# The first layer's image loop, with its barriers and semaphore clearing, written out as one block of straight code

## What is computed

```python
x_norm = _group_norm(x, gn_scale, gn_bias).reshape(b, seq, c)
qkv = x_norm @ w_qkv + b_qkv
q, k, v = jnp.split(qkv, 3, axis=-1)            # then to (b, 8, 1024, 64) each
weight = jax.nn.softmax(jnp.einsum('bhld,bhsd->bhls', q * scale, k * scale), axis=-1)
out = jnp.einsum('bhls,bhsd->bhld', weight, v)  # back to (b, 1024, 512)
out = out @ w_out + b_out
return (x_flat + out).reshape(b, h, w, c)
```

## Time and profile before

| | us |
|---|---|
| median of 3 runs | 4248.88 |
| the profiled execution | 4248.9 |
| its span (first to last instruction) | 4247.2 |
| VectorE busy | 2985.9 (70%) |
| ScalarE busy | 2580.8 (61%) |
| GpSimd busy | 1303.4 (31%) |

### The profile page before, as it was taken

The page is one execution under the profiler, slowest core; times in us unless marked ns, Lnnn a source line. Parts: engine busy times, 40 slices in busy tenths (PEclk is TensorE's granted clock), DMA queues, the critical chain, the costliest instruction groups (busy, mean ns, idle before and its releaser), DMA issues. The chain is left out here.

```text
span 4247.2 us, 65056 instructions
## 1 busy us (share of the span) xinstructions
PE 4062.9 (96%) x22762; PEld 3395.2 (80%) x22762; DVE 2985.9 (70%) x5141; ACT 2580.8 (61%) x5617; POOL 1303.4 (31%) x1423
## 2 busy tenths in 40 slices
PE   8999999999999999999999889999999999999999
PEld 6887878878878878788788577777777777777777
DVE  3983965956938839749569466859686868686866
ACT  3874855847828738558478136565656555555656
POOL 1431423432323324324323104132232314140504
PEclk9999999999999999999999989999999999999999
DMA  2221121221211211212211303031212121212212
GB/s 82 43 66 43 41 75 35 61 61 31 56 56 41 68 43 41 70 41 61 60 31 36 138 1 100 20 80 40 70 50 60 60 60 60 60 60 49 72 38 63
DMA packets 113159, 235.87 MB, mean 56 GB/s; under 512 B 17261, under 2 KB 33705, under 8 KB 112809
## 3 DMA queue, kind: packets, MB, share of 16 engines
q1 hardware_dynamic: 112808, 231.41, 20.4%
HBM read 80.35 MB, written 33.55 MB: 27 GB/s over the span
## 5 line engine op out<-in xcount | busy, mean ns | idle before, releaser
L599 DVE TENSOR_REDUCE a_neg_max<-a_ps 128x1 f32<-128x1024 f32 x512 | 624.7, 1221 | 337.1 <-PE a_ps L429 337.1
L558 ACT ACTIVATE a_ph<-a_ps 128x512 fp32r<-128x512 f32 x1024 | 556.9, 593 | 171.4 <-PE a_ps L443 168.5
L616 DVE TENSOR_TENSOR a_pl<-a_ps,a_ph 128x512 fp32r<-128x512 f32 x1024 | 654.2, 679 | 8.9 <-ACT a_ph L558 5.7
L565 ACT ACTIVATE a_prob<-a_ps,a_neg_max 128x1024 f32<-128x1024 f32 x512 | 572.3, 1118 | 17.5 <-DVE a_neg_max L599 11.8
L696 POOL TENSOR_TENSOR a_qk<-a_fold_s,a_fold_r 64x256 f32<-64x256 f32 x256 | 191.1, 747 | 1237.1 <-DVE a_fold_s L607 1237.1
L443 PEld LDWEIGHTS a_ps<-a_ident,a_prob 128*128 128x128 f32 x4096 | 469.8, 140 | 112.8 <-issue 47.0
L443 PE MATMUL a_ps<-a_ident,a_prob 128*128 128x128 f32 x4096 | 540.7, 274 | 17.3 <-DVE a_pl L616 16.2
L1697 POOL TENSOR_SCALAR b_prob<-b_prob,b_row_inv 128x256 f32<-128x256 f32 x512 | 246.7, 482 | 994.9 <-DVE b_row_inv L1606 959.0
L464 PE MATMUL a_ps<-a_ph,a_v 128*128 128x256 f32 x2048 | 550.7, 302 | 0.0
L464 PE MATMUL a_ps<-a_pl,a_v 128*128 128x256 f32 x2048 | 509.2, 282 | 0.0
L428 PE MATMUL a_ps<-a_kh,a_qs 128*128 128x512 f32 x1024 | 408.3, 399 | 11.9 <-POOL a_kl L687 11.9
(11 more groups left out here) (250 smaller groups left out, 9239.3 us busy)
## 6 DMA issues: line engine op xcount, KB each, us to landing
a_qs<-a_qk SPq DMA_DIRECT2D x128, 256.0 KB, 3.7
a_kl<-a_qk SPq DMA_DIRECT2D x128, 256.0 KB, 4.3
a_xtok<-in_x SPq DMA_DIRECT2D x64, 256.0 KB, 4.2
b_xs<-x SPq DMA_DIRECT2D x64, 256.0 KB, 4.6
b_qs<-b_qh SPq DMA_DIRECT2D x64, 256.0 KB, 3.0
b_qs<-b_ql SPq DMA_DIRECT2D x64, 256.0 KB, 3.8
b_z<-x SPq DMA_DIRECT2D x64, 256.0 KB, 3.2
out<-b_ot SPq DMA_DIRECT2D x64, 256.0 KB, 2.0
```

Of the source, the lines that this page charges most:

```text
L558: act.activation(ph[:, b % 2, 4 * g:4 * g + 4, (u % 2) * P:(u % 2 + 1) * P], ps[:, 4 + n % 2, :].rearrange("p (k q) -> p k q", k=4), ACT.C ...
L565: act.activation(prob[:, i_ % 2, :], ps[:, 2 * (i_ % 2):2 * (i_ % 2) + 2, :] .rearrange("p a b -> p (a b)"), ACT.Exp, bias=neg_max[:, i_:i ...
L599: dve.tensor_reduce(neg_max[:, i_:i_ + 1], ps[:, 2 * (i_ % 2):2 * (i_ % 2) + 2, :] .rearrange("p a b -> p (a b)"), AX, ALU.max, negate=Tru ...
L616: dve.tensor_tensor(pl[here], ps[:, 4 + n % 2, :].rearrange("p (k q) -> p k q", k=4), raw(ph[here]), ALU.subtract).then_inc(pl_ok, 1)
```

## The change

All eight images of the first layer stand in one block, each engine's list written out image by image. The functions of `image` become `sync_image(sp, r)`, `tensor_image(pe, r)` and so on, with a Python number `r` in place of the loop's register. The block's end per image (L364), the barrier with clearing per image (L716), the loop (L714) and the barrier behind the prologue (L360) are gone. The prologue's own block (and so its end, L262) stays, and so does the block's end and the clearing barrier behind the last image.

Semaphores are no longer cleared, so each wait asks for its count plus `r` times what an image adds (`EACH`). Where the barrier had covered an order between engines, a wait stands now: the matmuls of groups 4 to 7 wait until the previous image's output tile has left the bank, ScalarE waits for the four early groups' matmuls, for the previous image's last split before group 0, and for the previous image's stores before group 4.

```diff
-        def early(pe):
+        def early(pe, p):
             for k in range(CT):
-                pe.wait_ge(xh_ok, k + 1)
-                pe.wait_ge(xl_ok, k + 1)
+                pe.wait_ge(xh_ok, CT * p + k + 1)
+                pe.wait_ge(xl_ok, CT * p + k + 1)
                 for g in range(EARLY):
-                    project(pe, g, (k,))
+                    mm = project(pe, g, (k,))
+                    if k == CT - 1:
+                        mm.then_inc(pr_ps, 1)
...
-        nc.all_engine_barrier(sems_to_clear=range(min(nums), max(nums) + 1))
...
-        if n_images > 1:
-            with nc.Fori(0, n_images - 1) as i:
-                image(i, x[1:])
-                nc.all_engine_barrier(sems_to_clear=range(min(nums), max(nums) + 1))
-        image(n_images - 1)
+        EACH = {s.num: 16 for s in (*x_ld, *r_ld)}
...
+        EACH.update({s.num: 2 * U for s in (tr_ps, ph_ok, pl_ok)})
...
+        def counted(r):
+            return lambda sem, n: r * EACH[sem.num] + n
...
+            def projections(numbers):
+                for g in numbers:
+                    if g < 8 and r > 0:
+                        pe.wait_ge(out_ok, at(out_ok, g - 7))
+                    if g >= 8:
+                        pe.wait_ge(qk_sb, at(qk_sb, qk_upto[g - 7]))
...
+            def evict(g):
+                kind, m, s = groups[g]
+                act.wait_ge(pr_ps, at(pr_ps, g + 1))
+                if r > 0 and g == 0:
+                    act.wait_ge(al_ok, at(al_ok, 0))
+                if r > 0 and g == 4:
+                    act.wait_ge(o_st, at(o_st, 0))
...
+        with nc.Block() as block:
+            @block.sync
+            def _(sp):
+                for r in range(n_images):
+                    sync_image(sp, r)
+            @block.tensor
+            def _(pe):
+                for r in range(n_images):
+                    tensor_image(pe, r)
...
```

More of the change, by code:

```diff
@@ L324, in _ @@
                 pe.wait_ge(wql_ok, CT)
-                early(pe)
+                early(pe, 0)
             @block.vector
             def _(dve):
-                steps = [0]
                 def link(ins):
@@ L338, in _ @@
                     stats(dve, s)
-                moments(dve, link)
+                moments(dve, link, 0)
                 dve.wait_ge(pe_s, 1)
@@ L713, in layer0 @@
-        if n_images > 1:
-            with nc.Fori(0, n_images - 1) as i:
-                image(i, x[1:])
-                nc.all_engine_barrier(sems_to_clear=range(min(nums), max(nums) + 1))
-        image(n_images - 1)
+        EACH = {s.num: 16 for s in (*x_ld, *r_ld)}
+        EACH.update({s.num: TT for s in (xt_ps, xt_sb, bn_ok, vh_ok, vl_ok, out_ps, res_ok, out_ok)})
+        EACH.update({s.num: CT for s in (bn_ag, xn_ok, xh_ok, xl_ok)})
+        EACH.update({st_ok.num: 2, st_ps.num: 1, var_ok.num: 1, rstd_ok.num: 1})
@@ new lines, in layer0 @@
+        EACH.update({s_ld[0].num: 256, s_ld[1].num: 256, o_st.num: 16 * TT, pr_ps.num: len(groups), qk_sb.num: n_qk})
+        EACH.update({s.num: U for s in (score, max_ok, exp_ok, fold_cp)})
+        EACH.update({s.num: 2 * U for s in (tr_ps, ph_ok, pl_ok)})
+        EACH.update({s.num: U // 2 for s in (inv_ok, av_ps, fold_add, att_ok)})
+        EACH.update({staged.num: STAGE * NH, ah_ok.num: len(SPLIT_AT), al_ok.num: len(SPLIT_AT)})
+        def counted(r):
+            return lambda sem, n: r * EACH[sem.num] + n
@@ new lines, in sync_image @@
+        def sync_image(sp, r):
+            at = counted(r)
+            more = r + 1 < n_images
+            for h in range(NH):
+                p, j = h // 2, h % 2
+                sp.wait_ge(qk_sb, at(qk_sb, 4 if p == 0 else 4 + 4 * p))
+                if h >= 2:
+                    sp.wait_ge(score, at(score, TT * (h - 1)))
+                for half in range(2):
+                    rows_ = slice(HD * half, HD * half + HD)
+                    sp.dma_start(raw(qs[rows_, j, :]), qk[own_half(h), p, :]).then_inc(s_ld[j], 16)
+                    sp.dma_start(raw(kl[rows_, j, :]), qk[own_half(h), CT + p, :]).then_inc(s_ld[j], 16)
+            if more:
+                for j in range(2):
+                    sp.wait_ge(s_ld[j], at(s_ld[j], 64 * (NH // 2)))
+                for t in range(TT):
+                    sp.dma_start(xtok[:, t, :], x[r + 1, t * P:(t + 1) * P, :]).then_inc(x_ld[t], 16)
+            sp.wait_ge(score, at(score, U))
+            for t in range(TT):
+                if t == 2:
+                    sp.wait_ge(tr_ps, at(tr_ps, 2 * U))
+                if t == 6:
+                    sp.wait_ge(av_ps, at(av_ps, U // 2))
+                sp.dma_start(tok[t], x[r, t * P:(t + 1) * P, :]).then_inc(r_ld[t], 16)
+            for t in range(TT):
+                sp.wait_ge(out_ok, at(out_ok, t + 1))
+                sp.dma_start(x2[r, t * P:(t + 1) * P, :], tok[t]).then_inc(o_st, 16)
+            sp.wait_ge(o_st, at(o_st, 16 * TT))
@@ new lines, in tensor_image, with turn, scores, transposes @@
+        def tensor_image(pe, r):
+            at = counted(r)
+            more = r + 1 < n_images
+            def projections(numbers):
[4 more added lines that the diff above has]
+                        pe.wait_ge(qk_sb, at(qk_sb, qk_upto[g - 7]))
+                        if v_upto[g - 7]:
+                            pe.wait_ge(vl_ok, at(vl_ok, v_upto[g - 7]))
+                    project(pe, g).then_inc(pr_ps, 1)
+            def turn(tiles):
+                if more:
+                    for t in tiles:
+                        pe.wait_ge(x_ld[t], at(x_ld[t], 32))
+                        if t >= 4:
+                            pe.wait_ge(xt_sb, at(xt_sb, TT + t - 3))
+                        turn_tile(pe, t).then_inc(xt_ps, 1)
+            def scores(i_):
+                h, t = i_ // TT, i_ % TT
+                j = h % 2
+                if t == 0:
+                    pe.wait_ge(staged, at(staged, STAGE * (h + 1)))
+                if i_ < 2:
+                    pe.wait_ge(qk_sb, at(qk_sb, qk_upto[len(groups) - 8 + 2 * i_ + 2]))
+                else:
+                    pe.wait_ge(exp_ok, at(exp_ok, i_ - 1))
+                for kb in range(2):
+                    bank = ps[:, 2 * (i_ % 2) + kb, :]
+                    q_ = qs[:, j, t * P:(t + 1) * P]
+                    n = slice(kb * 512, (kb + 1) * 512)
+                    pe.matmul(bank, q_, kh[:, j, n], start=True, stop=False)
+                    mm = pe.matmul(bank, q_, kl[:, j, n], start=False, stop=True)
+                mm.then_inc(score, 1)
+            def transposes(u):
+                pe.wait_ge(exp_ok, at(exp_ok, u + 1))
+                if u == 0:
+                    pe.wait_ge(qk_sb, at(qk_sb, n_qk))
+                for g in range(2):
+                    n = 2 * u + g
+                    if n >= 2:
+                        pe.wait_ge(pl_ok, at(pl_ok, n - 1))
+                    for kk in range(4):
+                        kt = 4 * g + kk
+                        mm = pe.transpose(ps[:, 4 + n % 2, kk * P:(kk + 1) * P],
+                                          prob[:, u % 2, kt * P:(kt + 1) * P], ident[:])
+                    mm.then_inc(tr_ps, 1)
+            def output(b, part):
+                h = b // NB
+                if part == 0:
+                    pe.wait_ge(inv_ok, at(inv_ok, b + 1))
+                    if b == 0:
+                        pe.wait_ge(vl_ok, at(vl_ok, n_v))
+                    if b >= 2:
+                        pe.wait_ge(fold_add, at(fold_add, b - 1))
+                        pe.wait_ge(fold_cp, at(fold_cp, 2 * b - 2))
+                    for n in range(2):
+                        u = 2 * b + n
+                        pe.transpose(ps[:, 6 + b % 2, 256 + n * P:256 + (n + 1) * P],
+                                     row_inv[:, u:u + 1].to_broadcast([P, P]), ident[:])
+                pe.wait_ge(pl_ok, at(pl_ok, 4 * b + 3 + part))
+                for kt in range(4 * part, 4 * part + 4):
+                    for e, q_ in enumerate((ph, pl)):
+                        mm = pe.matmul(ps[:, 6 + b % 2, 0:256], v[:, h, kt, :], q_[:, b % 2, kt, :],
+                                       start=kt == 0 and e == 0, stop=kt == TT - 1 and e == 1)
+                if part == 1:
+                    mm.then_inc(av_ps, 1)
+            def out_tile(t):
+                if t == 0:
+                    pe.wait_ge(pl_ok, at(pl_ok, 2 * U - 1))
+                elif t == 1:
+                    pe.wait_ge(pl_ok, at(pl_ok, 2 * U))
+                elif t in (2, 3):
+                    pe.wait_ge(fold_add, at(fold_add, U // 2 + t - 3))
+                    pe.wait_ge(fold_cp, at(fold_cp, U + 2 * (t - 3)))
+                else:
+                    pe.wait_ge(out_ok, at(out_ok, t - 3))
+                n = slice(t * P, (t + 1) * P)
+                for k in range(CT):
+                    if k == 0 and t == 0:
+                        pe.wait_ge(ah_ok, at(ah_ok, SPLITS))
+                        pe.wait_ge(al_ok, at(al_ok, SPLITS))
```

(122 more changed lines are left out.)

440 lines of the change are left out of this document (111 added, 329 removed).

## The result

The changed kernel took 4201.52 us (median of 4 runs, 4199.93 to 4203.68), against 4249.32 us before (4 runs); the ratio is 0.9889, with a 95% interval of 0.9874 to 0.9903. The forecast was 4204 us, faster, in a range of 4197 to 4212. The profiled execution took 4202.9 us, 46.0 less than the one before; the sum had said 45.3.

The account below looks back on a forecast made before the run. TensorE, busy 96%, bounds the kernel, losing time to idleness and low clock at image seams. 29.8 + 1.4 + 0.7 + 12.8 + 0.6 = 45.3 us off 4248.9 gives about 4204 us, range 4197 to 4212.

Parts of the forecast that it names:

- The pause at the seams: TensorE's idleness between images goes: 29.8 us at six seams with a jump, 1.4 at the seam before image 7.
- The jump as the cause: At the first layer's seams, the taken branch must fetch its target (3.6 us), so the whole stop goes.
- Rival A: Straight code owes the fetch at the seams too; only 10.7 us go, low clock stays, 4238 us; 5%.
- The prologue's seam: Behind the prologue only the barrier L360 goes, the block's end stays; 0.7 us less.
- The low clock behind the seams and the slow restart: In the 216 matmuls behind seams, 1.2 GHz after idleness goes, 12.8 us; slower first matmuls at seven seams, 0.6 us.
- The added waits and the straight code: New waits on TensorE and ScalarE, and written-out images such as their attention stages, cost 0.
- Rival D: Instruction reads stop TensorE inside the written-out images; three stops of 3.6 us per image end at 4290 us; 3%.
- The low clock at the output tiles: The 2.2 us wait for VectorE stays in each image; one low-clock event follows, as before, priced at 1.57 us.
- rival B: Low clock follows the output-tile gap in four to seven images, giving back 5 to 9 us: 4208 to 4213; 15%.

Follow-up runs that it names:

- run 1: The kernel before with only its first layer's loop written out, block's end and clearing barrier kept at every seam; 4216.44 us, ratio 0.9928.
- run 5: The changed kernel with eight three-round loops added behind the first layer, bodies of 20 to 2000 transposes on TensorE; 6134.21 us in one run.
- run 3: The changed kernel with a pause of seven small GpSimd operations at each of seven seams, no branch or barrier; 4253.91 us, ratio 1.0009.
- run 4: The changed kernel with pauses growing from one to seven small GpSimd operations over the seams of images 1 to 7; 4233.26 us in one run.
- Run 7: The changed kernel with GpSimd's additions to output tiles 4 to 7 held back until VectorE has normalised two chunks; 4185.59 us, ratio 0.9853.

## Why the prediction was right, step by step

- **The pause at the seams** (31.2 us by the sum of its two parts): seven seams took 31.16 + 1.66 us before, and take 7 x 0.23 = 1.6 now. Right to 0.1 us. That no other wait took its place was the risk, and it did not come true: ScalarE evicts the first group at 329.10, and GpSimd has head 0 staged at 347.35 (344.95 + 2.40), 32 us ahead of its scores.
- **The jump as the cause** is shown by run 1 (33.2 us for the loop alone, with its low clock) and by run 5 (the distance, and the read of instructions within the long branch). Rival A, that straight code owes the same read at the seam, falls with the 0.23 us there. The words "a taken branch costs 3.6 us" would have been wrong for a short loop.
- **The prologue's seam** (0.7 us): 1.49 before, 0.71 after, 0.8 us.
- **The low clock behind the seams and the slow restart** (12.8 + 0.6 us): 405.43 - 391.76 = 13.7 us. That it was caused by the idleness was argued there from two seams; run 3 shows it for idleness of this length, and run 4 that shorter idleness is no sure sign.
- **The added waits and the straight code** (0): the seams stand at 0.23 us with the waits in them, and the attention stage is 0.03 to 0.05 us shorter, not longer. Rival D had nothing.
- **The low clock at the output tiles** (one event, as before): one event in the profiled execution, in image 5 and not in image 0; the other three executions have no profile. The count was right by luck as much as by reason. Run 1 has four, 6.2 us in all, and a changed kernel with seven would by this have taken some 4211 us. What spoke against rival B (one of seven) came from a kernel whose other six images each followed a slow stretch at their seam, so it was weak evidence for a kernel without these; the 15% look low.
- **What was not in the sum**: the layers' own parts. The first layer ends 45.9 us sooner (2364.51 to 2318.59, the last output matmul), the span is 47.0 us shorter, and the execution 46.0. The 1.1 us between the first two lies in the second layer, whose code is the same; its preparation took 1.7 us less, at a clock of 0.84 and not 0.83. From the last output matmul to the end of the span, code that nobody changed took between 1880.2 us (run 1) and 1884.5 us (run 4) in the profiles. That is the floor for any forecast of this kernel, and that the sum met the profiled execution to 0.7 us is partly luck. In the first layer alone the gain was 45.9 us, against 45.3 in the sum.

## What to carry to other kernels

Look at a loop's seam for what ends TensorE's idleness: if it is a branch of microseconds, the body was too long here (2000 matmuls and loads were, 1600 were not), and writing it out removed the read and the slow stretch behind it. The block's end and the barrier with clearing, which look like the expensive part in the code, were 0.5 and 0.65 us here, against 3.5 to 3.8 for the jump and 2.1 for the clock. Afterwards read the list of waits again: the longest wait that was left in each image went when one line was moved in another engine's order, which was worth 18 us.

## What the runs showed of the hardware

- A short operation with two SBUF inputs on VectorE can wait for one on GpSimd: 128x4 took 1.15 to 1.21 us beside a 128x512 addition on GpSimd and 0.16 to 0.17 us without one (the second such operation ended at 311.93, GpSimd's second addition at 311.91), and two normalisations of 128x1024 took 3.45 us against 1.54. The slowing goes both ways: two of GpSimd's additions took 2.53 us beside the small ones and 3.54 beside a split and what follows it. (The Trainium skill, "GPSIMD Engine Reference", Specifications, says that the two engines share their SBUF interfaces, with contention where VectorE has two SBUF inputs or a 2-port mode. Run 7 agrees for the small ones, which have two SBUF inputs.)
- A seam of 3.95 us left the clock at 2.4 GHz (granted clock 1.00 in the 216 matmuls behind it, once), and shorter stops (a seam of 3.25 us, or 2.2 us at the output tiles) were followed by 1.2 GHz for a while. What decides it was not settled.
- Bodies of up to 1600 matmul and load instructions were run again by TensorE without reading them again; with 2000 each round read them, and each taken branch took 3.3 us or more.
